# Attention probabilities split by ScalarE and GpSimd and turned by DMA in a four-block transformer kernel on one core

## What is computed

```python
q = (layernorm(x) @ Wq + bq)             # 16 heads of 32
k, v = split(context @ Wkv + bkv)        # 77 rows
scores = einsum('bhid,bhjd->bhij', q, k) * 32 ** -0.5
scores = where(mask, -inf, scores)
attn = softmax(scores, axis=-1)
out = einsum('bhij,bhjd->bhid', attn, v) @ Wout + bout
x = x + tanh(g_xattn[1]) * out
```

## Time and profile before

| | |
|---|---|
| median of three runs | 1818.28 us |
| profiled execution: time, span | 1823.66 us, 1821.9 us |
| TensorE, VectorE, ScalarE, GpSimd busy | 1371.2, 1421.6, 692.5, 243.9 us |
| mean granted clock of TensorE | 0.892 |
| DMA transposes L314, L344, L336 | 64, 32, 16 issues; 4.0, 4.9, 3.1 us to landing in the median |
| instructions | 24307 |

### The profile page before, as it was taken

How to read it: one execution, slowest core, us unless ns; L and a number is a source line. 1 busy time by engine, 2 the same in 40 slices (tenths; PEclk the granted TensorE clock), 3 DMA queues, 4 the chain that set the end, 5 groups by cost and what they waited for, 6 DMA issues and landing times.

```text
span 1821.9 us, 24307 instructions
## 1 busy us (share of the span) xinstructions
PE 1371.2 (75%) x8120; PEld 705.4 (39%) x8120; DVE 1421.6 (78%) x2437; ACT 692.5 (38%) x2105; POOL 243.9 (13%) x197
## 2 busy tenths in 40 slices
PE   5044737799787978698778978797869886988663
PEld 4021315344453436344543345343634453434321
DVE  6988896878787687787787878768777778786695
ACT  2112206451455227441644146422734164425310
POOL 1102200131003200230013100320013001310000
PEclk9556868899889989999999989998999999999888
DMA  9175761042101420233004210142023300420012
GB/s 348 68 243 146 188 143 36 6 88 64 42 1 35 93 59 14 35 62 77 25 7 87 58 48 1 35 93 59 14 35 65 75 24 6 87 58 24 7 24 51
DMA packets 267433, 120.08 MB, mean 66 GB/s; under 512 B 244090, under 2 KB 244602, under 8 KB 265750
## 3 DMA queue, kind: packets, MB, share of 16 engines
q1 hardware_dynamic: 267286, 118.27, 26.5%
HBM read 49.04 MB, written 8.39 MB: 32 GB/s over the span
## 4 chain that ended last, share of the span: by engine, by line
issue 43%; DVE 26%; PE 18%; DMA 4%; SPq 4%; ACT 3%; POOL 2%; POOLq 0%; DVEq 0%; ACTq 0%
PE bank L1075 13%; PE bank L1164 5%; DVE amax L826 2%; DVE pair L835 2%; DVE hid L831 2%; SPq L314 2%; DVE th L868 2%; SPq L303 1%; DVE pair L850 1%; DMA region<-region 1%; ACT region L535 1%; DVE pair L843 1%; DMA hqt<-pair 1%; DVE sc L797 1%; DVE stats L686 1%
## 5 line engine op out<-in xcount | busy, mean ns | idle before, releaser
L1164 PE MATMUL bank<-w_dn,region 128*128 128x512 fp8e4 x1024 | 243.7, 386 | 40.0 <-DMA region<-region 40.0
L1075 PE MATMUL bank<-w_up,xt 128*128 128x512 fp8e4 x1024 | 248.6, 391 | 32.7 <-ACT region L499 17.4
L1075 PE MATMUL bank<-w_gate,xqt 128*128 128x512 bf16 x512 | 147.9, 416 | 122.2 <-DVE th L868 78.4
L508 ACT ACTIVATE th<-bank,half_cg 128x512 f32<-128x512 f32 x128 | 88.0, 687 | 350.2 <-PE bank L1075 350.2
L426 POOL TENSOR_TENSOR region<-g,region 128x512 f16<-128x512 f32 x128 | 178.9, 1402 | 300.9 <-ACT region L499 292.9
L868 DVE SCALAR_TENSOR_TENSOR th<-th,bank 128x512 f32<-128x512 f32 x128 | 87.6, 684 | 138.4 <-ACT th L508 138.3
L535 ACT ACTIVATE region<-bank,nm 128x77 f32<-128x77 f32 x512 | 160.0, 345 | 68.2 <-DVE nm L914 68.2
L1075 PE MATMUL bank<-w_down,hqt 128*128 128x512 bf16 x512 | 134.3, 422 | 56.9 <-DMA hqt<-pair 56.9
L496 ACT ACTIVATE g<-bank 128x512 f32<-128x512 f32 x128 | 76.4, 597 | 247.2 <-PE bank L1075 188.2
L1164 PEld LDWEIGHTS bank<-w_dn,region 128*128 128x128 f16 x1024 | 101.0, 99 | 167.4 <-issue 52.0
L1075 PEld LDWEIGHTS bank<-w_up,xt 128*128 128x128 f16 x1024 | 102.0, 101 | 163.5 <-issue 55.4
(11 more groups left out here) (206 smaller groups left out, 2473.6 us busy)
## 6 DMA issues: line engine op xcount, KB each, us to landing
xin<-in_x SPq DMA_DIRECT2D x16, 512.0 KB, 4.1
out_x<-x SPq DMA_DIRECT2D x16, 512.0 KB, 3.0
region<-in_w_up_t SPq DMA_DIRECT2D x1, 4096.0 KB, 12.9
hid<-in_gate_w SPq DMA_DIRECT2D x4, 1024.0 KB, 5.2
x<-in_gate_w SPq DMA_DIRECT2D x4, 1024.0 KB, 6.1
hid<-in_up_w SPq DMA_DIRECT2D x4, 1024.0 KB, 5.2
x<-in_up_w SPq DMA_DIRECT2D x4, 1024.0 KB, 5.8
hid<-in_down_w SPq DMA_DIRECT2D x4, 1024.0 KB, 4.9
```

Of the source, the lines that this page charges most:

```text
L508: eng.activation(th[:, u % 2, :], bank[4][:, :], ACT.Tanh, scale=half_cg[:, :]).then_inc(sg["th"], 1)
L1075: last = mm(out, lhs, rhs, start=(n == 0), stop=(n == len(pairs) - 1))
L1164: last = mm(bank[2 + t % 2][:, :], ht[i][:, t % 2, f, :], w_dn[:, f, :], start=(f == 0 and i == 0), stop=(f == KF - 1 and i == 1))
```

## The change

- The float32 turns on TensorE (L1235) go. ScalarE now makes the float16 high part straight from the exponentials in SBUF, [128, 4, 77], one step after them; GpSimd (`p_lo`) subtracts it for the low part. Both lie side by side in one of three buffers `ps3`, [128, 2, 4, 128] of float16, of which 77 of each 128 columns are written.
- SyncE turns each such buffer with one DMA transpose, 128 x 1024 (`turn_p`), into one of four buffers `pt3`; two of these lie in `th`, which only the other phase uses. Sixteen of them stand in `turns` ahead of all else of the pass.
- The exponentials have no accumulator any more. The values get a 33rd column of ones (zeros in the low part), so the product with the values gives the row sums in its last column; it goes to two banks of eight heads. VectorE inverts and divides from there, in two halves.
- Scores have three banks (4, 5, 7), maxima and exponentials three buffers each. The score product of step n waits for the exponentials of step n - 3 instead of n - 2; exponentials wait for the low part of n - 3; ScalarE's copy waits for the landing of the transpose three steps earlier.
- The product with the values is at m + 5 instead of m + 4, and everything per tile behind it is one step later: lags 6, 7 (turn and copy), 8, 9, 10. The steps of the next group (norm, turns of x, `up`) and of the quantising stay where they are. On GpSimd the second norm's root comes between the residuals of steps 14 and 15.

```diff
@@ -47,6 +47,7 @@
...
+PV_LAG = 5
...
@@ -98,7 +99,7 @@
...
-        vals1 = [sb(f"vals1{i}", [M, B, D], F16) for i in range(2)]
+        vals1 = [sb(f"vals1{i}", [M, B, HEADS, HD + 1], F16) for i in range(2)]
...
@@ -143,16 +144,13 @@
...
-        at = 2 * KD * T + 4 * T
-        pt3 = [region[:, at + i * 2 * HC * P:at + (i + 1) * 2 * HC * P].rearrange("p (r h t) -> p r h t", r=2, h=HC)
-               for i in range(2)]
+        p3 = f32_at(2 * KD * T, 3 * HC * M).rearrange("p (r h m) -> p r h m", r=3, h=HC)
+        turn_n = 2 * HC * P
+        ps3 = [region[:, at:at + turn_n] for at in (half - 2 * turn_n, half - turn_n, 2 * half - 2 * turn_n)]
...
-        at = half + 2 * TILES * D
-        p3 = f32_at(at, 2 * HC * M).rearrange("p (r h m) -> p r h m", r=2, h=HC)
-        at += 4 * HC * M
+        pt3 = [region[:, at:at + turn_n] for at in (2 * half - 4 * turn_n, 2 * half - 3 * turn_n)]
...
-        assert at <= 2 * half - 2 * D
...
@@ -232,9 +232,21 @@
...
+        def want_pt(eng, g, m):
...
+            want(eng, f"pt{m % 4}", g, 16 * (m // 4 + 1))
...
+        def with_sums(a):
...
+            return bank[(2, 6)[a]][:, 0:HEADS // 2 * (HD + 1)].rearrange("p (h e) -> p h e", h=HEADS // 2)
...
+        def scores(n):
...
+            return bank[(4, 5, 7)[n % 3]]
...
@@ -328,6 +340,15 @@
...
+            def turn_p(g, m):
+                want(sp, "p3l", g, m + 1)
+                sp.sem_inc(sm["sp_passed"])
+                if m >= 4:
+                    want(sp, "o3", g, m - 3)
+                    sp.sem_inc(sm["sp_passed"])
+                sp.dma_start_transpose(pt3[m % 4].rearrange("p i h t -> p (i h) t"),
+                                       ps3[m % 3].rearrange("p i h t -> p (i h t)")).then_inc(sg[f"pt{m % 4}"], 16)
...
@@ -348,6 +369,8 @@
...
+                for m in range(TILES * NC):
+                    turn_p(g, m)
...
                     turn_x(g, h)
...
@@ -407,10 +430,19 @@
...
+            def p_lo(g, m):
...
+                want(pool, "p3h", g, m + 1)
+                eng.tensor_tensor(ps3[m % 3][:, 1, :, 0:M], p3[:, m % 3], ps3[m % 3][:, 0, :, 0:M],
+                                  ALU.subtract).then_inc(sg["p3l"], 1)
...
-                if g1 is not None:
-                    want(pool, "var2", g1)
-                    eng.tensor_tensor(sdev[:, :, :], ve2[:, :, :], powers[:, :, :], ALU.pow).then_inc(sg["rstd2"], 1)
+                for n in range(STEPS):
+                    if g3 is not None and 2 <= n <= TILES * NC + 1:
+                        p_lo(g3, n - 2)
+                    if n == VAR2_AT + 1 and g1 is not None:
+                        want(pool, "var2", g1)
+                        eng.tensor_tensor(sdev[:, :, :], ve2[:, :, :], powers[:, :, :], ALU.pow).then_inc(sg["rstd2"], 1)
...
@@ -518,24 +550,21 @@
...
-                if 2 <= n <= TILES * NC + 1:
-                    m = n - 2
-                    want(act, "p3t", g, m + 1)
-                    if m >= 2:
-                        want(act, "o3", g, m - 1)
-                    eng.activation(pt3[0][0:M, m % 2], bank[6 + m % 2][0:M, :].rearrange("p (h t) -> p h t", h=HC),
-                                   ACT.Copy).then_inc(sg["p3h"], 1)
...
                     want(act, "nm3", g, n + 1)
-                    if n >= 2:
-                        want(act, "p3t", g, n - 1)
-                    t, c = divmod(n, NC)
+                    if n >= 3:
+                        want(act, "p3l", g, n - 2)
...
-                        h = HC * c + j
-                        last = eng.activation(p3[:, n % 2, j, :], bank[4 + n % 2][:, j * M:(j + 1) * M], ACT.Exp,
-                                              bias=nm3[:, n % 2, j:j + 1], accum_out=rs3[:, t % 2, h:h + 1])
+                        last = eng.activation(p3[:, n % 3, j, :], scores(n)[:, j * M:(j + 1) * M], ACT.Exp,
+                                              bias=nm3[:, n % 3, j:j + 1])
...
-                t = tile_at(n, 6)
+                if 1 <= n <= TILES * NC:
+                    m = n - 1
+                    want(act, "p3", g, m + 1)
+                    if m >= 3:
+                        want_pt(act, g, m - 3)
+                    eng.activation(ps3[m % 3][:, 0, :, 0:M], p3[:, m % 3], ACT.Copy).then_inc(sg["p3h"], 1)
+                t = tile_at(n, 7)
...
@@ -658,10 +687,12 @@
...
+            for i in range(2):
+                done(eng.memset(vals1[i][:, :, :, HD:HD + 1], 1.0 - i))
...
-                split(vals1[0][:, b, :], vals1[1][:, b, :], sq[0:M, :])
+                split(vals1[0][:, b, :, 0:HD], vals1[1][:, b, :, 0:HD], sq[0:M, :].rearrange("p (h e) -> p h e", h=HEADS))
...
@@ -900,35 +931,30 @@
...
-                t = tile_at(n, 5)
+                t = tile_at(n, 6)
...
-                    eng.tensor_tensor(on3[:, :].rearrange("p (h e) -> p h e", h=HEADS),
-                                      bank[2][:, :].rearrange("p (h e) -> p h e", h=HEADS),
-                                      rr3[:, :].unsqueeze(2).to_broadcast([P, HEADS, HD]),
-                                      ALU.mult).then_inc(sg["on3"], 1)
+                    for a in range(2):
+                        hs = slice(a * HEADS // 2, (a + 1) * HEADS // 2)
+                        done(eng.reciprocal(rr3[:, hs].unsqueeze(2), with_sums(a)[:, :, HD:HD + 1]))
+                    settle()
+                    for a in range(2):
+                        hs = slice(a * HEADS // 2, (a + 1) * HEADS // 2)
+                        eng.tensor_tensor(on3[:, :].rearrange("p (h e) -> p h e", h=HEADS)[:, hs], with_sums(a)[:, :, 0:HD],
+                                          rr3[:, hs].unsqueeze(2).to_broadcast([P, HEADS // 2, HD]),
+                                          ALU.mult).then_inc(sg["on3"], 1)
...
-                    eng.tensor_reduce(nm3[:, n % 2, :], bank[4 + n % 2][:, 0:HC * M].rearrange("p (h m) -> p h m", h=HC),
+                    eng.tensor_reduce(nm3[:, n % 3, :], scores(n)[:, 0:HC * M].rearrange("p (h m) -> p h m", h=HC),
...
-                if 3 <= n <= TILES * NC + 2:
-                    m = n - 3
-                    want(dve, "p3h", g, m + 1)
-                    eng.tensor_tensor(pt3[1][0:M, m % 2], bank[6 + m % 2][0:M, :].rearrange("p (h t) -> p h t", h=HC),
-                                      pt3[0][0:M, m % 2], ALU.subtract).then_inc(sg["p3l"], 1)
-                t = tile_at(n, 3)
-                if t is not None:
-                    want(dve, "p3", g, NC * t + NC)
-                    done(eng.reciprocal(rr3[:, :], rs3[:, t % 2, :]))
-                    settle()
-                t = tile_at(n, 7)
+                t = tile_at(n, 8)
...
-                t = tile_at(n, 9)
+                t = tile_at(n, 10)
...
@@ -1205,44 +1231,37 @@
...
-                    if n >= 2:
-                        want(pe, "p3", g, n - 1)
+                    if n == 2:
+                        want(pe, "nm3", g, 1)
+                    if n >= 3:
+                        want(pe, "p3", g, n - 2)
...
-                    product(bank[4 + n % 2][:, 0:HC * M],
+                    product(scores(n)[:, 0:HC * M],
...
-                if 4 <= n <= TILES * NC + 3:
-                    m = n - 4
+                if PV_LAG <= n < TILES * NC + PV_LAG:
+                    m = n - PV_LAG
...
-                    want(pe, "p3l", g, m + 1)
+                    want_pt(pe, g, m)
...
-                        want(pe, "on3", g, t)
+                        want(pe, "on3", g, 2 * t)
...
-                        es = slice(h * HD, (h + 1) * HD)
-                        last = product(bank[2][:, es], [(pt3[0][0:M, m % 2, j, :], vals1[0][:, b, es]),
-                                                        (pt3[0][0:M, m % 2, j, :], vals1[1][:, b, es]),
-                                                        (pt3[1][0:M, m % 2, j, :], vals1[0][:, b, es])])
+                        hi, lo = (pt3[m % 4][0:M, i, j, :] for i in range(2))
+                        last = product(with_sums(h // 8)[:, h % 8, :], [(hi, vals1[0][:, b, h, :]), (hi, vals1[1][:, b, h, :]),
+                                                                       (lo, vals1[0][:, b, h, :])])
                     last.then_inc(sg["o3"], 1)
-                if 2 <= n <= TILES * NC + 1:
-                    m = n - 2
-                    want(pe, "p3", g, m + 1)
-                    if m >= 2:
-                        want(pe, "p3l", g, m - 1)
-                    for j in range(HC):
-                        last = tr(bank[6 + m % 2][0:M, j * P:(j + 1) * P], p3[:, m % 2, j, :], ident[:, :])
-                    last.then_inc(sg["p3t"], 1)
-                t = tile_at(n, 6)
+                t = tile_at(n, 7)
...
-                    want(pe, "on3", g, t + 1)
+                    want(pe, "on3", g, 2 * t + 2)
...
                     last.then_inc(sg["ott"], 1)
-                t = tile_at(n, 8)
+                t = tile_at(n, 9)
...
```

More of the change, by code:

```diff
@@ L78 @@
 WT_DONE = WT_AT[-1]
-DVE_STEPS = 141
+DVE_STEPS = 145
 RADD = bass.bass_isa.ReduceOp.add
```

(2 more changed lines are left out.)

8 lines of the change are left out of this document (4 added, 4 removed).

## The result

The changed kernel is slower: 1846.81 us in the median of four runs (1846.27 to 1848.7) against 1817.03 for the kernel before, a ratio of 1.0164 (95% interval 1.0141 to 1.0186). The forecast was 1750 with a range of 1712 to 1800, and a chance of 0.10 for slower. The profiled execution of after took 1848.7 us around a span of 1846.6, 24.7 more than the span of before.

The account below looks back on a forecast made before the run. TensorE and ScalarE were taken to bind the mixed score loops almost equally, ScalarE the last pass. Seven mixed passes saving 7 + 2 us each, plus 3.4 and 1.5, gave 68 off the 1818.28 median: 1750, range 1712 to 1800.

Parts of the forecast that it names:

- A: Score loops: GpSimd near its high row and longer landings give 2.3 us a step; 1802 us, chance 10%.
- C: Score loops: DMA turns do not overlap, each step pays 3.2 us, 48 us per loop; 1907 us, chance 3%.
- (d): Mixed pass's tail: two residuals between the normalisation steps leave VectorE, 0.6 us each at the most.
- (b): Mixed pass's tail: last output turn moves behind second ternary product; wait before the third grows by up to 1.9 us.
- (a): Mixed pass's tail: tile 2's output product moves behind the last turns of x, over evictions; gain 1.1 to 3.7 us.
- (c): Tail: last quantising step moves ahead of last residual sum, 0.7 us off VectorE's chain, L336 transpose about 4 us earlier.
- (e): Mixed pass's tail: last residual on GpSimd slows VectorE's four normalising instructions; 0.6 us lost, between 0 and 1.7.
- (f): Mixed pass's tail: last turn of probabilities lands some 8.9 us after the last maximum starts; hidden, otherwise costs 3 us.
- the loop's factor: Mixed loops: largest load 24.2 us times 1.16 (35.8 for a load of 30.9 before), taken as 28.8; 7 us saved each.
- Rival B: Mixed loops: less TensorE work lowers its clock; at 0.60 a loop takes 40.3 us; 1831 us total, chance 8%.
- The last pass: Eighth pass, without the next group's first attention beside it: 3.4 us saved in its loop, 1.5 in its tail.
- the ring's estimate: Score loop: ScalarE copy, GpSimd residual, transpose landing, copy three steps later; 1.6 us a step, 24.0 for 15 steps.

Follow-up runs that it names:

- e2: The change, with the second norm put ahead of tile 1's residual sum on VectorE in mixed passes: 1813.46 us, ratio 0.9944.
- e1: The change with the old lags back (value product four steps after the scores, tile steps at 5 to 9): 1810.85 us, ratio 0.9923.
- e3: The kernel before with only the one-step shift of lags and a third buffer of turned probabilities: 1859.99 us, ratio 1.0209.
- e4: The change plus four unread float32 turns on TensorE ahead of each step's scores: 1851.21 us, ratio 1.0173.
- e8: The kernel before without row sums: exponentials have no accumulator, the division uses 1: 1807.83 us, ratio 0.9937.
- e7: e1 with ScalarE's copy of the probabilities in the same step as their exponentials: 1783.26 us, ratio 0.9814.
- e10: e7 plus four unread float32 turns on TensorE in each of steps 3 to 8: 1783.68 us, ratio 0.98.

## Why the prediction was wrong, step by step

**The durations were right.** Exponentials every 0.21 us; the copy 0.47 to 0.50 (predicted 0.50); GpSimd's residual 0.75 (0.8), between 747 and 760 ns in all 128; landings 3.0 to 3.1 (3.1) and overlapping, issued at 1.23 each. TensorE's load in the loop was put at 24.2; the third pass shows 26.7, but 9 us of it ran at the low clock, where eight products take 3.33 us instead of 1.89; the first pass, at a clock of 0.96, shows 24.8 us. VectorE's 20.7 was measured as 20.5, ScalarE's 24.1 as 22.4. Rivals A and C, a slow ring and turns that don't overlap, are out. The Trainium skill's figure for the crossbar in "VectorE: DVE Perf Modes", section "The three transpose paths", is 1309 ns for one square. The prediction's estimate from it, eight times as long for eight squares or 10.5 us, did not come true: eight squares took SyncE 1.23 us to issue and landed 3.1 us after it.

**The step that failed first: the tail.** The prediction went through the parts that lag 10 moves and named tile 2's output product and tile 3's turn, but not tile 1: its residual sum at step 17, ahead of the norm in VectorE's order, and behind an output product that waits for a late copy. It priced (d) as 0.6 us off VectorE's path each, for residuals that stood between the normalisation's steps, and did not look at what the shift put there instead. Predicted -2 us, measured +5.4; e2 gives 3.0 of that back with one swap, e1 all of it, and e3 finds 4.3 of it in a kernel without the rest of the change. The prediction also had no term for a lower clock in the tail. It was 1.00 in four of seven passes and fell to 0.84 in all, and in the third pass tile 1's output product took 1.7 us more. How much of the tail beyond e2's 3.0 is clock and how much order stays open. Of the named parts, (b) was right: the wait ahead of the third ternary product grew from 1.45 to 3.18. (a) was not: tile 2's output product (739.60 to 743.17) did move behind the turns of x, but stands directly ahead of the first ternary product and takes 3.6 us there, more than the 1.98 of idle time that it was to fill. The ternary product starts 18.2 us after the last maximum, where about 15 was forecast; before, it is 17.6 in the pass that was read and 15.0 in the third, whose clock is 1.00. (c) was right: TensorE enters the gate at 756.83 with no idle time. (e) cost nothing: the last residual runs ahead of the norm (729.92), whose instructions take 542 ns each as before (541). (f) was right: the value products of the last turns wait for nothing in the tail. Also, the pass that was read, the second, has the longest tail of the kernel before (29.5 us; four of the seven have 25.2), so it was a poor sample for that part.

**The second: the loop's factor.** The prediction took the largest load (24.2 us) times 1.16, 28.1, raised it to 28.8 because three loads were nearly equal, and so forecast 7 saved; the loop took 33.2 and saved 2.4. The factor spread the waits evenly over the loop, where they stand in few places. By an estimate from the rows of the third pass, two of them make up the missing 4.6 us. First, the two intervals at the first output product are chains between engines: 5.5 and 3.2 us in after, 4.2 and 3.4 before, 3.7 and 2.8 in e1 with the old lags, 5.6 and 3.8 in e3 with the shift alone. The shift made them 2.1 us longer (8.6 against e1's 6.6). Second, the low clock fell on three intervals that take 8.2 us in after and 5.7 in e2, so 2.5 us. (e1, with the shorter of these chains, pays 3.05 us for its first landing instead.) Where neither stands, the load was a good guide: the intervals from the 10th to the 12th maximum shrank from 2.1 and 2.5 us to 1.6 and 1.9, by the 0.48 that the turns took from TensorE and a little more, and e4 puts 0.4 to 0.5 of it back. ScalarE's shorter exponentials alone, in e8, save 1.7 us a loop, but the savings of the two don't add up in an interval that both bind. (From start to start the first and the seventh loop of before take 35.2 us; the 35.8 and 35.7 in the earlier trace rows are windows that also hold the last maximum itself.)

**Rival B was half right.** Its mechanism, less work and a lower clock, did occur, at 0.85 and not at the 0.64 from which it would have decided alone. After's first loop against the next five (31.1 at 0.96, 33.7 at 0.85) puts its price at 2.6 us where it strikes, e7's two kinds of loop at 2.8. It was priced as a rival, with 8%, where it should have been a term of the forecast, and its place was given as the loops alone. The measured 1846.81 lies beyond even B's 1831, because the tail, which B did not name, lost the most.

**The last pass** was right in sign and a little large: 3.5 saved from its first maximum to the end of the kernel instead of 4.9. Its loop gained 1.6 instead of 3.4, since filling the longer pipeline costs one interval of 5.7 us (the wait for the first landing) that the ring's estimate left out. Behind the loop, 1.9 were saved up to the end of the kernel (1.5 predicted): the gate started 26.6 us after the last maximum instead of 27.6, as (c) had it, although the last residual sum came 4.6 later (26.8 us against 22.2; 22.1 in e7).

**What stays open.** The rest of the period (134.6 us before) is 135.5 in after, up to 136.7 in e4 and down to 133.7 in e10, and why was not isolated. Nor is it shown why the clock differs between passes of one program, nor how e2's swap reached the clock of the loop that follows. No run holds the tail's clock fixed while the order changes. No kernel combined e7 with further moves of the output product.

## What to carry to other kernels

When a change deepens a software pipeline by one step, list every item that the shift moves past a fixed one on each in-order engine; here one residual sum ahead of one norm decided the sign (+1.6% with it, -0.6% without). If a longer latency makes the extra step seem necessary, first shorten the way up to it: the copy in the same step let the old lags stand and turned the change into -1.9%. And work taken off an engine saves time only in the intervals that this engine bounds: price a loop interval by interval, by what ends each, and not by the largest load times a factor. A lower clock costs time by where it falls, so look for its place and not for its mean.

## What the hardware showed that was not expected

TensorE's granted clock was 0.50 for 9 us behind a stretch in which it was idle for 2.13 and 1.73 us and busy 2.86 of 5.7; with the unread turns of e4 it was busy 4.24 of 5.7 there and kept 1.00 in what followed:

```profile
697.20:702.90 5.70, 4.24 (x42) 3.33 (x43) 3.20 (x8) 5.18 (x21) 1.50 (x2) 1.00 0.17 36
702.90:711.90 9.00, 7.83 (x96) 6.14 (x97) 4.69 (x13) 6.87 (x29) 3.31 (x5) 1.00 0.90 130
```

Putting back as unread work what a change had taken away moved the kernel by 0.1 points (1.0164 to 1.0173), less than the intervals of the two; in the loop the clock gave back in one place what the work cost in another. GpSimd's residual from SBUF to SBUF held 747 to 760 ns beside everything else, though its subtraction in the earlier trace rows reaches 2992. An exponential of 77 columns on ScalarE without the accumulator read follows the last after 0.21 us instead of 0.29.
